# A graph convolution on one core: four instead of three of 13 edge tiles fetched by one-hot products, all picks made by two-tensor compares

## What is computed

```python
src = concat([s, d, arange(3125)]); dst = concat([d, s, arange(3125)])   # 103125 edges, sorted by dst
# etypes: 16 relations, weight: 16 x 64 x 64, x: 3125 x 64

h = feat[src]
for r in range(16):
    m = m + where(etypes == r, 1, 0)[:, None] * (h @ weight[r])
out = segment_sum(m, dst, 3125)
x = layernorm(x + out)      # over the 64 features, no scale, no shift
```

## Time and profile before

| what | us |
|---|---|
| median of 3 runs | 871.02 (870.95 to 871.26) |
| span of the profiled execution | 870.6 |
| POOL busy | 591.7 (68%) |
| PE busy / weight loads | 684.9 (79%) / 643.7 (74%) |
| DVE busy | 598.9 (69%) |
| ACT busy | 585.6 (67%) |
| before the first gather | 70.8 |
| mean granted TensorE clock | 0.967 of full |

### The profile page before, as it was taken

How to read it: one execution, slowest core, us unless ns; L and a number is a source line. 1 busy time by engine, 2 the same in 40 slices (tenths; PEclk the granted TensorE clock), 3 DMA queues, 4 the chain that set the end, 5 groups by cost and what they waited for, 6 DMA issues and landing times.

```text
span 870.6 us, 24502 instructions
## 1 busy us (share of the span) xinstructions
PE 684.9 (79%) x8136; PEld 643.7 (74%) x8137; DVE 598.9 (69%) x2220; ACT 585.6 (67%) x1326; POOL 591.7 (68%) x634
## 2 busy tenths in 40 slices
PE   0004998888889888888898888889888888898894
PEld 0004888787878877887887788779877887798784
DVE  0146886767677776777678668766876687678754
ACT  1307777776777677677777777677777677777732
POOL 2005777777777777777777777777777777777760
PEclk9999899999999999999999999999999999999996
DMA  1022222222222222222222222222222222222211
GB/s 63 38 88 64 71 74 69 69 63 72 69 66 66 69 72 63 69 69 71 64 66 72 69 63 69 71 70 61 71 69 72 60 72 69 71 61 69 54 46 39
DMA packets 30272, 57.46 MB, mean 66 GB/s; under 512 B 11402, under 2 KB 19402, under 8 KB 30258
## 3 DMA queue, kind: packets, MB, share of 16 engines
q0 software_dynamic: 19840, 40.67, 19.6%
q1 hardware_dynamic: 9102, 15.55, 5.0%
q10 hardware_dynamic: 1316, 1.06, 0.4%
HBM read 54.84 MB, written 2.40 MB: 66 GB/s over the span
## 4 chain that ended last, share of the span: by engine, by line
POOL 61%; issue 25%; SPq 5%; DMA 4%; PE 2%; ACT 1%; DVE 1%; POOLq 0%; DVEq 0%; ACTq 0%
POOL rows L286 61%; DMA src_b<-in_src 4%; SPq L218 2%; SPq L217 2%; PE own L686 1%; ACT away L374 1%; DVE outT L571 1%; PE own L825 0%; PE rel L736 0%; PE agg L724 0%; POOLq L194 0%; DMA rows<-x_parts,gidx 0%; ACT pick L380 0%; DVE x_sb L600 0%; ACT krel L404 0%
## 5 line engine op out<-in xcount | busy, mean ns | idle before, releaser
L286 POOL DMA_INDIRECT rows<-x_parts,gidx x620 | 586.0, 945 | 244.0 <-issue 188.0
L686 PE MATMUL own<-xp,pick 125*128 125x192 bf16 x4650 | 412.8, 253 | 82.5 <-issue 74.6
L686 PEld LDWEIGHTS own<-xp,pick 125*128 125x128 bf16 x4650 | 397.2, 101 | 93.9 <-issue 83.9
L464 DVE TENSOR_SCALAR pick<-src_h,node 125x384 bf16<-125x384 f16 x1240 | 401.9, 402 | 8.4 <-ACT src_h L342 8.4
L528 DVE TENSOR_SCALAR onehot<-ramp,krel 128x112 bf16<-128x112 bf16 x806 | 149.4, 262 | 49.6 <-issue 49.6
L374 ACT ACTIVATE away<-src_h,node_neg 125x384 bf16<-125x384 f16 x310 | 169.6, 613 | 0.1
L380 ACT ACTIVATE pick<-away,one 125x384 bf16<-125x384 bf16 x310 | 163.0, 610 | 0.0
L724 PE MATMUL agg<-onehot,rows 128*128 128x112 bf16 x2418 | 139.8, 215 | 29.1 <-DMA rows<-x_parts,gidx 23.8
L724 PEld LDWEIGHTS agg<-onehot,rows 128*128 128x128 bf16 x2418 | 122.4, 99 | 48.2 <-issue 48.1
L388 ACT ACTIVATE rows<-own 128x192 bf16<-128x192 f32 x186 | 61.4, 330 | 138.9 <-PE own L686 131.7
L736 PE MATMUL rel<-aggT,w_pair 128*64 128x64 f32 x992 | 128.7, 298 | 0.0
(11 more groups left out here) (62 smaller groups left out, 72.6 us busy)
## 6 DMA issues: line engine op xcount, KB each, us to landing
src_b<-in_src SPq DMA_DIRECT2D x62, 187.5 KB
rows<-x_parts,gidx POOLq DMA_INDIRECT x620
x_parts<-xp SPq DMA_DIRECT2D x1, 812.5 KB
x_parts<-xp SPq DMA_DIRECT2D x1, 750.0 KB
out<-x_sb SPq DMA_DIRECT2D x2, 250.0 KB
x_sb<-in_x ACTq DMA_DIRECT2D x1, 406.2 KB
src_i<-in_src SPq DMA_DIRECT2D x1, 396.5 KB
dst_i<-in_dst SPq DMA_DIRECT2D x1, 396.5 KB
```

The lines of the kernel that those rows point to most:

```text
L286: pool.indirect_dma_start(rows[:, u, j, :], None, x_parts, bass.IndirectOffsetOnAxis(ap=gidx[:, u, j:j + 1], axis=0)).then_inc(rows_in[u] ...
L464: v.tensor_scalar(pick[u][:, b, :], src_h[u][:, :, 0:CUTW[u]], node[:, b:b + 1], None, ALU.is_equal).then_inc(pick_ready[u], 1)
L686: return nc.tensor.matmul(own[h][:, 0:SPLIT * D], pick[u][:, b, h * P:(h + 1) * P], xp[:, b, 0:SPLIT, :].rearrange("p s d -> p (s d)"), st ...
```

## The change

`OWN` goes from (3, 3) to (4, 4), so POOL gathers nine tiles of each group instead of ten, and PE fetches four. The results of two tiles share one PSUM bank, and ACT copies them out in pairs. DVE makes all 25 blocks of `pick`, in five instructions of five blocks each; each compares two tensors (the source numbers repeated over the blocks, and a table `node` of node numbers repeated 64 times). ACT makes none. The gaps in the source numbers and in `ramp` are gone. `relate` runs once a turn, for both groups together, on twice the columns, and a turn later. The loops are written in another order.

```diff
-    OWN = (3, 3)
+    OWN = (4, 4)
...
-    CUT = 3
-    CUTW = [-(-n * P // (2 * CUT)) * 2 for n in OWN]
-    OWNW = [CUT * w for w in CUTW]
-    GAP = 2
-    APICK = 5
-    VPICK = NB - APICK
+    OWNW = [n * P for n in OWN]
+    RUN = 64
+    PIECES = 5
+    PB = NB // PIECES
...
-        ramp = sb("ramp", [P, WIN, R + GAP], bf16)
-        node = sb("node", [NP, NB])
+        ramp = sb("ramp", [P, WIN, R], bf16)
+        node = sb("node", [NP, NB, RUN], f16)
...
-        src_h = [sb(f"src_h{u}", [NP, CUT, CUTW[u] + GAP], f16) for u in range(2)]
+        src_h = [sb(f"src_h{u}", [NP, OWNW[u]], f16) for u in range(2)]
...
+            def take_own(i, u):
+
+                for k in range(OWN[u] // 2):
+                    act.wait_ge(own_done[u], i * OWN[u] + (2 * k + 2))
+                    pair = own[k][:, :].rearrange("p (h c) -> p h c", h=2)
+                    act.activation(rows[:, u, 2 * k:2 * k + 2, 0:SPLIT * D], pair[:, :, 0:SPLIT * D], ACT.Copy).then_inc(own_rows[u], 1)
+                    act.activation(rows[:, u, 2 * k:2 * k + 2, SPLIT * D:RP * D], pair[:, :, 0:D], ACT.Copy).then_inc(own_rows[u], 1)
...
                 if more:
                     narrow_sources(i + 1, 0)
+                take_own(i, 1)
+                take_agg(i, 0)
+                if more:
                     group_indices(i + 1, 0)
-                take_agg(i, 0)
-                take_own(i, 1, lambda h: act_picks(i + 1, 0, h) if more else None)
-                if more:
-                    act_picks(i + 1, 0, 3)
-                if more:
                     narrow_sources(i + 1, 1)
-                    group_indices(i + 1, 1)
+                    take_own(i + 1, 0)
                 take_agg(i, 1)
                 if more:
-                    take_own(i + 1, 0, lambda h: act_picks(i + 1, 1, h))
-                    act_picks(i + 1, 1, 3)
+                    group_indices(i + 1, 1)
...
-                for b in range(VPICK):
-                    v.tensor_scalar(pick[u][:, b, :], src_h[u][:, :, 0:CUTW[u]], node[:, b:b + 1], None, ALU.is_equal).then_inc(pick_ready[u], 1)
+                for n in range(PIECES):
+                    b0 = n * PB
+                    v.tensor_tensor(pick[u][:, b0:b0 + PB, :].rearrange("p b (r e) -> p b r e", e=RUN),
+                                    src_h[u][:, :].rearrange("p (o r e) -> p o r e", o=1, e=RUN).to_broadcast([NP, PB, OWNW[u] // RUN, RUN]),
+                                    node[:, b0:b0 + PB, :].rearrange("p b (o e) -> p b o e", o=1).to_broadcast([NP, PB, OWNW[u] // RUN, RUN]),
+                                    ALU.is_equal).then_inc(pick_ready[u], 1)
...
-                    last = v.tensor_scalar(onehot[:, u, j, :], ramp[:, :, 0:R],
+                    last = v.tensor_scalar(onehot[:, u, j, :], ramp[:, :, :],
...
+            def relate(i):
+
+                for u in range(2):
+                    pe.wait_ge(agg_copied[u], i * 3 + 3)
+                if not is_first(i):
+                    pe.wait_ge(rel_added, i * 4)
+                av = aggT[:, :, :, :].rearrange("d u n r -> d (u n) r")
                 for q in range(RQ):
-                    last = nc.tensor.matmul(rel[0:D, 0:2 * SPAN], w_pair[:, q, :], aggT[:, u, :, q],
+                    last = nc.tensor.matmul(rel[0:D, 0:4 * SPAN], w_pair[:, q, :], av[:, :, q],
                                             start=(q == 0), stop=(q == RQ - 1))
```

More of the change, by code:

```diff
@@ L26, in gnn_resnorm @@
     GT = 13
-    OWN = (3, 3)
+    OWN = (4, 4)
     LATE = GT - 3
-    assert max(OWN) <= 3
+    assert max(OWN) <= 4 and all(n % 2 == 0 for n in OWN)
     HALF = (0, 7, GT)
@@ L50, in gnn_resnorm @@
     RP = SPLIT + 1
-    CUT = 3
-    CUTW = [-(-n * P // (2 * CUT)) * 2 for n in OWN]
-    OWNW = [CUT * w for w in CUTW]
-    GAP = 2
-    APICK = 5
-    VPICK = NB - APICK
+    OWNW = [n * P for n in OWN]
+    RUN = 64
+    PIECES = 5
+    PB = NB // PIECES
+    assert PB * PIECES == NB and P % RUN == 0
     XHALF = (0, 13, NB)
@@ L396, in _ @@
             narrow_sources(0, 0)
-            act.wait_ge(const_set, 5)
-            for part in range(3):
-                act_picks(0, 0, part)
             act.wait_ge(krelT_done, 1)
@@ L572, in add_x, with turn @@
                 dve.wait_ge(xT_taken, XT)
[L574 to L589 removed]
+            dve.wait_ge(out_zeroed, 1)
+            def turn(i):
+                picks(i + 1, 0)
+                if not is_first(i):
+                    add_rel(i - 1)
+                onehots(i + 1, 0)
+                picks(i + 1, 1)
+                onehots(i + 1, 1)
             group_loop(dve, turn, last=LAST)
@@ L592, in _ @@
                             AX.X, ALU.max).then_inc(any_set, 1)
-            turn(LAST, more=False)
+            dve.wait_ge(again_done[0], 1)
+            dve.wait_ge(again_done[1], 1)
+            take_mean(x_sb, x_mean, x_centered, NB)
+            add_rel(LAST - 1)
+            add_x()
+            add_rel(LAST)
             def finish(n):
```

150 lines of the change are left out of this document (39 added, 111 removed).

## The result

| kernel | median us (lowest to highest) | ratio to before, 95% interval |
|---|---|---|
| before | 870.99 (870.18 to 871.26) | |
| changed | 895.17 (885.96 to 902.47) | 1.0238 (1.0182 to 1.0294) |
| changed, timed again beside other kernels | 897.53 (891.2 to 898.8), before 872.02 | 1.0282 (1.0244 to 1.032) |

The changed kernel is slower by 2.4%. This ratio leaves out the longest of its four runs (902.47 us), which counts as slow because it lies over 1.5% above the shortest; with it the medians are 2.8% apart. The forecast was 5.2% slower, so its direction was right and its size twice too large. The profiled execution is the longest of the four (span 900.7). The runs of this kernel lie further apart than those of before; the waits of the gathers, shown in the next rows, also differ from run to run.

What follows compares the result with a forecast made beforehand. POOL's gathers bound the kernel before; afterwards PE 25.5, POOL 25.0 and DVE with ACT nearly level, plus 0.8 of waits, make 26.3 us a turn: 870.6 + 39.9 + 5 = 915.5 us, so 916, range 895 to 945.

Steps and rivals of the forecast that it cites:

- The bound of before: POOL before the change: twenty gathers, one every 1.248 us, make 24.97 us, exactly a turn, so POOL sets the pace.
- Compares: DVE's picks: a two-tensor compare of 2560 elements lasts 1.48 us, five last 7.0 us and ten 14.0.
- Relation products: PE: 16 a turn of 128 columns instead of 32 of 64, still 3.9 us; the halved count saves nothing.
- narrow relation products: Rival: a record costs the same at 128 columns; PE's turn 23.6 us; with free gathers 835 us; chance of faster 0.12.
- The shared port: Gathers beside DVE compares with two SBUF inputs go at 1.50 instead of 1.25 us, ten a turn; POOL needs 25.0 us.
- PE's gaps: PE's register loads and loop jump, partly hidden behind queued products: 0.9 us a turn, within a PE turn of 25.5.
- The coupling: PE, POOL and DVE with ACT each wait a little for the others: 0.8 us more, 26.3 us a turn.
- Start and end: First aggregation behind both first fetches, last relation products twice as wide: 5 us for both (3 to 10).
- No contention: Rival: compares do not delay gathers, PE alone decides at 25.5 us a turn, 891 us; chance 0.15 for 885 to 895.
- Long waits: Rival: a gather waits for all five compares, POOL's turn about 35 us, 1185 us; chance 0.20 together with two-port one-hots.
- One element per cycle: Rival: compares last 2.82 us, DVE becomes the bound at 33 us a turn, 1120 us; chance 0.05.
- Two-port one-hots: Rival: one-hots with dense `ramp` exclude gathers too, 1 to 3 us a turn, 945 to 1005 us; chance 0.20 with long waits.

Runs made afterwards that it cites:

- set A: The first eight follow-up runs, variants of both kernels, made where the kernel before took 1365 to 1392 us at a mean granted clock of 0.74 to 0.76.
- set B: The later follow-up runs, variants of both kernels, some of them repeats, made where the kernel before took 872 us.

## Why the prediction was right in direction and wrong in size

**The bound of before**: right. POOL's 20 gathers were the turn.

**Compares**: 1.48 us forecast, 1485 ns measured; five in 7.10 (7.0 forecast). Right.

**Relation products**: 3.9 us a turn forecast; from 450.00 to 453.84 they take 3.84, 240 ns a record. Right: the halved count saves nothing, and "narrow relation products" falls.

**The shared port**: right in kind, and the step that decides, but priced too low. Ten gathers a turn are delayed, 2.5 us a turn forecast; 95.4 us in 29 turns are 3.3. What was missing is the gather that asks just after a burst has begun: it waits 1.30 us, and 43 of them lie in those turns. The forecast had the same wait in its hands, 0.8 us in the earlier trace rows, and priced only what follows once the two are in step. That gathers get in at each change at all was an assumption ("If one waiting gather gets through"). It came true in this kernel, where DVE has a pause ahead of nearly every burst; the run on the kernel before with two-tensor compares shows the other case, so here the forecast had some luck.

**PE's gaps: the first wrong term.** The forecast had 0.9 us a turn, 0.1 to 0.2 measured. The loads and the jump hide behind queued products, as in the turns of 24.61 us. PE's turn is 24.6 and not 25.5.

**The coupling: the term that failed.** "Each waits a little for the others. I add 0.8 us" put 26.3 on top of PE's 25.5. It rested on two things. One was a PE turn longer than POOL's; it is shorter. The other was that a gather delays a compare by 0.1; it does not: five compares take 7.10 us in each burst beside gathers, and 7.08 in the one that lets none in. With one engine never idle, the turn is that engine's: 18 gathers at 1.434 on average are 25.8, and 25.62 was measured, since the 29 turns hold 518 gathers, 17.9 a turn. Forecast 26.3 for 25.62 is 29 x 0.68 = 19.7 us too many. The forecast's own 25.0 for POOL, without the allowance, would have been 0.6 too few.

**Start and end**: outside of the 29 turns the changed kernel needs 900.7 - 743.1 = 157.6 us and the one before 870.6 - 29 x 24.97 = 146.5, so 11.1 more; 5 + 1.3 (the thirtieth turn) were forecast, 4.8 too few. The gather of 7.59 us is 6.6 of it. The two misses partly cancel by luck. Measured less forecast, they are -19.7 and +4.8, together the 14.8 us between 915.5 and 900.7 but for rounding; the median lies 7 us below the time of the profiled run (902.47). Fewer long waits would explain it, but of those runs no trace was kept.

**Rivals.** "No contention" (891) comes close in number and is wrong in kind: PE alone, by the 24.6 us of work it really has, would be faster than before in every turn, 29 x 0.36 = 10 us. "Long waits" happened once in each profiled run of the changed kernel, not in every burst; with compares straight behind one-hots they are the rule (59 of 60 bursts in set A), so this rival was closer than its chance says. "One element per cycle": with both inputs in SBUF it did not come (1485 ns); 2815 ns, what that rival said, is what the compare takes with an input in PSUM. Two-port one-hots: at most 0.1 us for some gathers, as said above. The clock was 1.00 in the turns, as forecast; before, one turn in three had 0.93 (the earlier trace rows show one such turn).

## What to carry to other kernels

Where GpSimd issues indirect DMAs without a pause, look for DVE's instructions with two SBUF inputs beside them. A gather that meets one waits. In the better case it waits for the end of that one, and its cycle is rounded up to whole instructions, so their length against the gather's own 1.22 us matters more than their sum. In the worse case, seen where the burst starts straight behind one-hots, it waits for the whole burst. So look in the trace which case it is, and what DVE does ahead of the burst. When one engine is never idle, its list is the time; add no allowance for the others on top, but do allow for the phase in which its waits begin. And move work off the bounding engine only up to the point where the next one is full: one tile more in every second group gave 2.3% with the change's loops and the picks as they were; one more in each was a loss with either kind of picks.

## What the hardware showed that was not expected

- Once per run of the changed kernel, in the second burst, a gather sat out all five compares: 7.59 us here, 7.47 to 7.77 in the other profiles of set B with two-tensor compares (7.65 with six compares). In all other bursts gathers got in at changes. With two-tensor compares straight behind one-hots in nearly every group (the kernel before, set A) a gather sat out the burst, or what was left of it, in 59 of 62. Why stays open.
- Shorter compares are worse where gathers get in between them: at a pitch of 1.14 us gathers came every 2.27, at 1.40 every 1.40.
- A two-tensor compare loses half its rate with a float32 operand in PSUM (2815 against 1485 ns for 2560 elements), though it frees the gathers. Whether the type or the place halves it was not separated.
- In set A, PE's instruction stream stood still for 0.16 to 0.89 us every few products, and the same kernel took 1365 to 1392 us instead of 871. The number of the chip on record is 12 for all of set A, and also 12 for three runs of set B (four blocks, half the relation products, and the picks of before with (4, 3)), so if the number names one chip, it is a condition and not the chip. Why the changed kernel suffers less (1202), the runs do not show.
